# Routed rows' layernorm in halves: statistics split across two chunks, scaling and modulation spread over later steps

## The reference

```python
mod = (silu(c) @ wmod).reshape(B, 6, 1, D)        # sa, ca, ga, sb, cb, gb; ga, gb clamped away from 0
h = layernorm(x) * (1 + ca) + sa
x = x + ga * attention(h)                          # window 128, causal, 16 heads
h = layernorm(x) * (1 + cb) + sb                   # the routed rows
logits = h @ gate_w.T + gate_b; probs = softmax(logits); top 2
for each choice: token -> slot expert*CAP + position, dropped beyond CAP
    hmid = relu(xbuf @ W1 + b1); y += (hmid @ W2 + b2)[slot] * prob
x = x + gb * y
```

## Time and profile before

| | |
|---|---|
| median of 3 runs | 1144.18 us (1142.86 to 1144.82) |
| the profiled execution | 1141.23 us, its span 1139.4 us |
| mean granted TensorE clock | 0.997 of full |
| chunks 1 to 5 | about 84.4 us each |

### The profile page before, as it was taken

The page is one execution under the profiler, slowest core; times in us unless marked ns, Lnnn a source line. Parts: engine busy times, 40 slices in busy tenths (PEclk is TensorE's granted clock), DMA queues, the critical chain, the costliest instruction groups (busy, mean ns, idle before and its releaser), DMA issues.

```text
span 1139.4 us, 25547 instructions
## 1 busy us (share of the span) xinstructions
PE 1092.5 (96%) x9548; PEld 718.3 (63%) x9548; DVE 818.5 (72%) x1767; ACT 676.0 (59%) x1892; POOL 481.0 (42%) x541
## 2 busy tenths in 40 slices
PE   7999999999999999999998998899999999999996
PEld 4455655655655655655655566566776768585865
DVE  6766596596596686587577688797786868687755
ACT  5677486486477477477376475547474564727361
POOL 2243254354354355255245265445344352534342
PEclk9999999999999999999999999999999999999999
DMA  9753000100100000000300004374446363534000
GB/s 334 144 170 118 20 1 20 38 2 25 34 1 29 29 2 30 28 1 29 88 12 34 20 11 129 105 147 78 110 92 156 69 144 105 121 107 83 22 20 10
DMA packets 109715, 77.46 MB, mean 68 GB/s; under 512 B 72842, under 2 KB 100634, under 8 KB 109340
## 3 DMA queue, kind: packets, MB, share of 16 engines
q1 hardware_dynamic: 98844, 54.32, 19.7%
q0 software_dynamic: 10752, 21.54, 6.5%
HBM read 49.99 MB, written 33.78 MB: 74 GB/s over the span
## 4 chain that ended last, share of the span: by engine, by line
PE 85%; DVE 5%; ACT 3%; POOL 2%; issue 2%; DMA 1%; SPq 1%; DVEq 0%; POOLq 0%; ACTq 0%
PE up L1614 16%; PE down L1640 16%; PE gen L556 15%; PE score L593 7%; PE gen L570 7%; PE gen L647 6%; PE pt L604 6%; PE pv L624 6%; PE pv L631 4%; ACT prob L864 1%; SPq L1539 1%; POOL slot_inputs L1399 1%; ACT h L832 1%; DMA slot_inputs<-hT,send 0%; ACT h2T L898 0%
## 5 line engine op out<-in xcount | busy, mean ns | idle before, releaser
L1389 POOL TENSOR_SCALAR_AFFINE_SELECT probT_split<-probT 128x512 f32<-128x512 f32 x128 | 99.1, 774 | 304.1 <-ACT probT L872 300.3
L1666 ACT ACTIVATE hid<-up,b1T 128x512 f16<-128x512 f32 (+1 forms) x192 | 122.2, 636 | 175.5 <-PE up L1614 171.4
L1614 PE MATMUL up<-xT,w 128*128 128x512 f16 (+1 forms) x1152 | 210.6, 343 | 5.9 <-DVE xT L1523 3.5
L1640 PE MATMUL down<-w,hid 128*128 128x256 f16 x1920 | 213.7, 273 | 2.3 <-DVE hid L1682 1.3
L1640 PEld LDWEIGHTS down<-w,hid 128*128 128x128 f16 x1920 | 187.1, 98 | 27.8 <-DVE hid L1682 2.7
L556 PE MATMUL gen<-hT,big 128*128 128x512 f16 x768 | 186.5, 382 | 7.4 <-ACT h2T L898 4.3
L864 ACT ACTIVATE prob<-score,negmax 128x128 f32<-128x128 f32 x512 | 180.6, 374 | 0.7 <-DVE negmax L1050 0.7
L1614 PEld LDWEIGHTS up<-xT,w 128*128 128x128 f16 x1152 | 112.5, 98 | 99.0 <-DVE xT L1523 3.6
L1762 POOL DMA_INDIRECT out<-y,tail x80 | 85.9, 1074 | 187.4 <-DVE y L1712 174.2
L1682 DVE TENSOR_TENSOR hid<-hid 128x512 f16<-128x512 f32 (+1 forms) x192 | 112.2, 604 | 55.7 <-ACT hid L1667 55.6
L872 ACT ACTIVATE probT<-pt 128x512 f32<-128x512 f32 x128 | 76.9, 600 | 91.7 <-PE pt L604 91.7
(11 more groups left out here) (163 smaller groups left out, 1533.9 us busy)
## 6 DMA issues: line engine op xcount, KB each, us to landing
slot_inputs<-empty_row SPq DMA_DIRECT2D x80, 129.5 KB, 2.5
raw<-slot_inputs SPq DMA_DIRECT2D x28, 320.0 KB, 5.7
big<-in_L_ffn_W SPq DMA_DIRECT2D x28, 256.0 KB
big<-in_L_ffn_W SPq DMA_DIRECT2D x7, 1024.0 KB
out<-x SPq DMA_DIRECT2D x7, 512.0 KB, 2.9
x<-in_L_attn_x SPq DMA_DIRECT2D x1, 3072.0 KB, 23.3
kept<-out,tail POOLq DMA_INDIRECT x80, 3.4
out<-y,tail POOLq DMA_INDIRECT x80, 2.5
```

Of the source, the lines that this page charges most:

```text
L1389: pool.affine_select(out=probT_split[:, h % 2, :, 1], in_=probT[:, h % 2], pattern=[[0, TILES], [1, P]], compare_op=ALU.is_ge, fill=zero, ...
L1614: mm = pe.matmul(bank, w1[:, par, kd, a, ft * P:(ft + 1) * P], part_rows(e, n, xT[:, par, b * KD + kd, :]), start=(i == 0), stop=(i == 5))
L1640: mm = pe.matmul(down[bank][:, s, :], hid[:, ft, a, t * P:(t + 1) * P], w2[:, par, ft, b, :], start=(i == 0), stop=(i == 3 * FT - 1))
L1666: act.activation(part_rows(e, n, hid[:, ft, 0, :]), bank, ACT.Relu, scale=1 / W_SCALE, bias=bias).then_inc(hid_hi, 1)
```

## The change

The statistics of a round 1 to 6 are made two tiles at a time. The first two tiles' statistics stand at the end of the preceding chunk, between `ln_second` and the second addition; the other two at step 4. Scaling is done by halves in steps 4 and 6 (before: all four tiles in step 5), modulation by halves in steps 7 and 8 (before: 6 and 8). GpSimd's `reciprocal_std` stays at step 5 and waits for both halves; `stats_made` counts them. The last chunk's rounds 7, 8 and 9 keep their steps; only the numbers of semaphores that they wait for are new.

```diff
-            def reciprocal_std(pool, mv, rs, mv_sem, var_sem, rs_sem, n, tiles=slice(0, TILES)):
-                stand_ge(pool, (mv_sem, n))
+            def reciprocal_std(pool, mv, rs, mv_sem, var_sem, rs_sem, n, tiles=slice(0, TILES), made=None):
+                stand_ge(pool, (mv_sem, made or n))
...
-            ROUTE_AT = {"stats": 4, "rstd": 5, "scale": 5, "shift_by_half": (6, 8), "token": 8, "pack": 9, "low": 9,
+            ROUTE_AT = {"stats": 4, "rstd": 5, "scale_by_half": (4, 6), "shift_by_half": (7, 8), "token": 8, "pack": 9, "low": 9,
...
+            def stats_made(r):
+
+                return 2 * r if r < LAST else LAST + r - 1
...
+                    def half_stats(r, half):
                         c, t0, nt, rows_out = route_round(r)
+                        dve.wait_ge(x2_ready, 2 * c + half + 1)
+                        norm_stats(dve, c * TILES, stats[1], meanvar[1], r_stat, r_mv, stats_made(r) - 1 + half, range(2 * half, 2 * half + 2))
+
+                    def part_scale(r, half=None):
+                        c, t0, nt, rows_out = route_round(r)
+                        dve.wait_ge(r_mv, stats_made(r))
+                        for s in range(t0, t0 + nt) if half is None else range(2 * half, 2 * half + 2):
                             op = dve.scalar_tensor_tensor(h2[:, s, :], x[:, c * TILES + s, :], meanvar[1][:, s, 0:1],
                                                           modrow[:, batch(c), 2, :], ALU.subtract, ALU.mult)
-                        op.then_inc(r_xn, 1)
+                        if half != 0:
+                            op.then_inc(r_xn, 1)
...
-                            if not first and i == at["stats"]:
+                            if last and i == at["stats"]:
                                 part_stats(c)
-                            if not first and i == at["scale"]:
+                            if not first and not last and i == at["stats"]:
+                                half_stats(c, 1)
+                            if last and i == at["scale"]:
                                 part_scale(c)
+                            if not first and not last and i in at["scale_by_half"]:
+                                part_scale(c, at["scale_by_half"].index(i))
...
                             add_attention(c, 0)
                             if c + 3 < NC:
                                 ln_second(c + 3)
+                            if c + 1 < LAST:
+                                half_stats(c + 1, 0)
                             add_attention(c, 1)
...
-                                reciprocal_std(pool, meanvar[1], rstd[1], r_mv, r_var, r_rstd, c)
+                                reciprocal_std(pool, meanvar[1], rstd[1], r_mv, r_var, r_rstd, c, made=stats_made(c))
```

More of the change, by code:

```diff
@@ L1201, in part_stats @@
                         dve.wait_ge(x2_ready, 2 * r if r < NC else 2 * c + r - NC + 1)
-                        norm_stats(dve, c * TILES, stats[1], meanvar[1], r_stat, r_mv, r, range(t0, t0 + nt))
-                    def part_scale(r):
+                        norm_stats(dve, c * TILES, stats[1], meanvar[1], r_stat, r_mv, stats_made(r), range(t0, t0 + nt))
+                    def half_stats(r, half):
                         c, t0, nt, rows_out = route_round(r)
-                        dve.wait_ge(r_mv, r)
-                        for s in range(t0, t0 + nt):
+                        dve.wait_ge(x2_ready, 2 * c + half + 1)
[4 more added lines that the diff above has]
+                        for s in range(t0, t0 + nt) if half is None else range(2 * half, 2 * half + 2):
                             op = dve.scalar_tensor_tensor(h2[:, s, :], x[:, c * TILES + s, :], meanvar[1][:, s, 0:1],
                                                           modrow[:, batch(c), 2, :], ALU.subtract, ALU.mult)
-                        op.then_inc(r_xn, 1)
+                        if half != 0:
+                            op.then_inc(r_xn, 1)
                     def part_modulate(r, half=None):
@@ L1417, in chunk @@
                             if last and i == EARLY_AT["rstd"]:
-                                reciprocal_std(pool, meanvar[1], rstd[1], r_mv, r_var, r_rstd, NC, slice(0, 2))
+                                reciprocal_std(pool, meanvar[1], rstd[1], r_mv, r_var, r_rstd, NC, slice(0, 2), stats_made(NC))
                             if last and i in SEND_AT:
@@ L1441, in attention_gpsimd @@
                     scatter(NC, range(2 * K))
-                    reciprocal_std(pool, meanvar[1], rstd[1], r_mv, r_var, r_rstd, NC + 1, slice(2, 4))
+                    reciprocal_std(pool, meanvar[1], rstd[1], r_mv, r_var, r_rstd, NC + 1, slice(2, 4), stats_made(NC + 1))
                     registers["last_token"] = pool.to_reg(T - 1)
```

## The result

The changed kernel takes 1148.46 us (median of 7 runs, 1146.48 to 1149.72), the kernel before 1143.29 (7 runs, 1141.26 to 1144.82): 1.0047 times as long, 95% interval 1.0037 to 1.0056, or +5.2 us between the medians. Forecast were 1148.1 and, as a difference, +3.9. It is slower, as forecast. The difference is 1.3 us larger than the forecast sum, and the median of the kernel before is 0.9 lower than that of the three runs known then. The profiled execution took 1147.34, its span 1145.5.

The account below looks back on a forecast made before the run. TensorE, busy 96% of the span, was taken as the bound. Six new waits of 1.25 us (+7.5) less 3.6 in chunk 6 gave +3.9, on 1144.18 us 1148.1; range 1143 to 1153.

Parts of the forecast that it names:

- The step that decides: First modulation half moved to odd step 7 delays `attn_low(1)`: a new TensorE wait of 1.25 us in six steps 8.
- The price of the pair: Two modulations on VectorE in step 7: 1.62 us beside GpSimd's selects (1.55 to the next start), 0.88 with GpSimd idle.
- The steps costed at nothing: Statistics at the chunk's end, scaling leaving step 5 in chunks 1 to 5, second scaling half at step 6: cost 0.
- Chunk 6's gain: Step 6 of chunk 6: the 2.08 us wait shrinks to about 0.1 and the low clock goes, gain 3.6 us.
- the base's: Starting time of the kernel before, to which the forecast difference was added: 1144.18 us.
- Not given back: The 1.25 us wait of step 8 is not recovered later, since nothing downstream was waiting for anything but TensorE.
- The clock rival: The 1.25 us waits of step 8 also bring the low clock, up to 1158.2 us if all six; chance 0.12.
- The other three: Selects out of the way, 1143.6 us, chance 0.10; no new wait, 1140.6, 0.10; chunk 6's gain fails, 1149.7 to 1151.7, 0.08.

Follow-up runs that it names:

- e6: Changed kernel with both modulation halves in step 7, none in step 8: 1158.01 us, +15.8 against before.
- e7: Changed kernel with step 7's modulation pair ahead of that step's merge instead of behind its normalisation: 1144.78 us, +1.7 against before.
- e4: Changed kernel with every `attn_low` moved from the start of an even step to behind the preceding odd step's normalisation, ahead of its routing work: 1141.04 us, -1.9 against before.
- e1: Kernel before with only the modulation halves moved, to steps 7 and 8 from 6 and 8: 1149.92 us, +7.2 against before.
- e2: Changed kernel with scaling back in step 5 and modulation in 6 and 8, only the split statistics left: 1143.48 us, +0.3 against before.
- e5: Kernel before with every `attn_low` moved behind the preceding odd step's normalisation, ahead of its routing work: 1141.71 us, -1.6 against before.
- e3: Changed kernel with scaling halves in steps 4 and 5 and modulation halves in 6 and 8: 1141.08 us, -1.3 against before.
- e8: Changed kernel with `attn_low` in odd steps between the row maximum and the normalisation: 1143.36 us, +0.7 against before.

## Why the prediction was right, and where a term was off

**The step that decides held.** A pair put into an odd step holds back `attn_low`, for which TensorE waits in the even one: 1.25 us in each of six chunks. Step 8 is longer by 1.24; doubling the work in front gives 1.97 to 2.08 (e6), cheapening it 0.52 (e7), moving `attn_low` ahead of it none (e4), and doing this part of the change alone +7.2 us (e1).

**The price of the pair held**: 1.62 us beside the selects, 1.55 to the next start, both as forecast; e7 shows the other bound, 0.88.

**The steps costed at nothing held, all but one.** As forecast were the statistics in the idle time, the second addition no later, the second scaling half in step 6 as long as the modulation it replaced, VectorE back in step by step 9. The exception: the prediction says that in chunks 1 to 5 TensorE was not held up in step 6, and calls these chunks equal. In chunk 4 the four scalings of step 5 did hold `attn_low(0)` back a little: it ended at 398.16, and the weighted values started at 398.31. Step 6 of chunk 4, TensorE, lasted 3.80 us before

```profile
397.41 0.77 PE L593 MATMUL score<-k,q 64*64 64x64 f32 x16
...
401.21 0.88 PE L593 MATMUL score<-k,q 64*64 64x192 f32 x16
```

and lasts 3.61 now:

```profile
401.12 0.78 PE L597 MATMUL score<-k,q 64*64 64x64 f32 x16
...
404.73 0.88 PE L597 MATMUL score<-k,q 64*64 64x192 f32 x16
```

**Chunk 6's gain was mis-sized.** The wait of 2.08 went, as forecast, and step 6 takes 3.71. But the prediction booked a gain of 3.6 us, the low clock behind the wait included, from one trace. Behind a wait of 2 us the clock fell in 3 of 11 cases: 1 of 3 traces of before, none in e1 and e2, 2 of 6 in e6. So the kernel before pays 2.1 us there (its step 6 lasts 5.87 in the second trace), and now and then 1.7 more. The sum with that is 6 x 1.25 - 2.1 = +5.4, or +5.2 with chunk 4's 0.2; measured are +5.2 between medians, +5.4 by the ratio, and 501.38 - 496.17 = +5.2 by the stages. That the absolute 1148.1 came within 0.4 us was luck: this error (1.5) and the base's (0.9 too high) have opposite signs.

**"Not given back" is not settled beyond the stage.** The prediction says that nothing downstream waited for anything but TensorE. Before the first expert's second part TensorE waits for VectorE's transposed rows in every trace, and less long in the changed kernel. The times (+5.4, 4.2 to 6.4) show that most of the cost remains.

**The rivals.** The clock rival did not come true: behind the 18 waits of 1.2 to 1.3 in the three traces (changed twice, e1) it never fell. The evidence that the prediction had against it was thin: the earlier trace rows shows the stretch that holds the 1.15 us wait and not the one behind it, and behind that wait the clock did fall in 2 of 13 traces. The other three are excluded by the rows above: the selects lie beside the pair, the new wait is there, and chunk 6's wait is gone. The low clock of step 18 in the first trace of the changed kernel, 1.4 us of its stage, was absent in the second; it also came in e5, behind the same wait (1.14).

**The faster version** is e4, -1.9 us against before and -7.3 against the changed kernel; e5, with nothing but the move of `attn_low` (-1.6), and e3, with the modulation back in even steps (-1.3), can't be told from it by their intervals.

**Open:** what decides whether the clock falls behind one of two equal waits was not found. e4 has two low stretches between 690 and 726 us in both traces, and e7 and e8 have two there, where the second and third traces of the kernel before have one and the first none; whether that is chance or belongs to the edits, so few traces don't tell.

## What to carry to other kernels

In a queue written by hand, ask of each instruction that you move what stands next behind it and which engine waits for that one. Here equal work was free in the even steps, behind `attn_low`, and cost 7.5 us in the odd ones, ahead of it. Where work stands in front of a short instruction that another engine waits for, move the short one ahead of it, and no further: one place further ahead, the next consumer paid (e8). And before a saving is booked as wait plus low clock, look at a second trace.

## What the runs showed of the hardware

Waits of TensorE of equal length are not followed by the same clock. Behind waits of about 2 us (1.97 to 2.09) in the stage the granted clock fell to 0.50 (1.2 GHz) in 3 of 11 cases, for some 3.4 us, and cost some 1.7 us each; behind the 18 single waits of 1.2 to 1.3 us it never fell; behind the 1.15 us wait of step 18, which stands behind shorter ones, it fell in 2 of the 13 traces that have it. In the first expert's products it stayed full behind a wait of 3.52 us in the first trace of the kernel before, and fell behind 4.18 and 4.47 in the other two and behind 2.97 in e4's first. All traces but that first one have one or two such stretches between 690 and 729 us, where the attention stage ends and the first expert starts.

The same two instructions of VectorE took 0.88 us with GpSimd idle, 1.24 and 1.62 beside its selects, and a normalisation took 2.50 instead of 0.68 when it met GpSimd's subtraction of 2.08 us (e8).
